# A two-layer transformer kernel on one core: new hand-made orders for every engine's work, with VectorE and GpSimd SBUF operations placed apart

## The reference, cut to what matters

```python
# layer 0: 8 query heads, 1 key/value head of 64, rotary embedding, SwiGLU of 2048
h = ada_rms(x, t, ln1_w, ln1_tw)        # n * (w * (1 + t @ tw.T))
q, k, v = h @ Wq.T, h @ Wk.T, h @ Wv.T
x = x + softmax(rope(q) @ rope(k).T / 8) @ v @ Wo.T
h = ada_rms(x, t, ln2_w, ln2_tw)
x = x + (silu(h @ Wg.T) * (h @ Wu.T)) @ Wd.T
# layer 1: 16 heads of 32, unit-length q and k, gates and shifts from the condition, GELU MLP of 2048
gamma1, gamma2, scale1, scale2, shift1, shift2 = silu(cond) @ Wada.T + bada
x = x + attn(_ln(x) * (scale1 + 1) + shift1) * gamma1
h = gelu_tanh((_ln(x) * (scale2 + 1) + shift2) @ Wfc1.T + bfc1)
x = x + (h @ Wfc2.T + bfc2) * gamma2
```

## Time and profile before

| | |
|---|---|
| median of 3 runs | 2560.11 us (2558.06 to 2566.29) |
| profiled execution | 2554.55 us, span 2552.8 us |
| mean granted clock of TensorE | 0.985 |
| busy: PE, DVE, ACT, POOL | 2449.8, 1422.2, 912.4, 1050.4 us |
| share of the DMA engines by the main queue | 35.8% |

### The profile page before, as it was taken

One profiled execution on the slowest core, in us unless ns is written; L12 is line 12 of the kernel. 1 busy time (PEld: TensorE's weight loads), 2 busy tenths in 40 slices (PEclk: granted clock), 3 DMA queues, 4 the chain that ended last, 5 costly groups with the idle time before them and its releaser, 6 DMA issues.

```text
span 2552.8 us, 46385 instructions
## 1 busy us (share of the span) xinstructions
PE 2449.8 (96%) x17878; PEld 1169.3 (46%) x17878; DVE 1422.2 (56%) x2062; ACT 912.4 (36%) x1496; POOL 1050.4 (41%) x943
## 2 busy tenths in 40 slices
...
GB/s 180 211 149 65 104 46 86 62 50 92 35 98 52 61 84 30 106 44 143 100 93 131 155 49 143 54 126 63 103 106 41 143 62 100 96 77 120 50 92 29
DMA packets 311504, 231.81 MB, mean 91 GB/s; under 512 B 227718, under 2 KB 238342, under 8 KB 311308
## 3 DMA queue, kind: packets, MB, share of 16 engines
q1 hardware_dynamic: 311308, 228.89, 35.8%
...
## 4 chain that ended last, share of the span: by engine, by line
PE 59%; POOL 16%; issue 12%; DVE 8%; ACT 3%; DMA 2%; SPq 1%; POOLq 0%; ACTq 0%; DVEq 0%
PE ps_m L1882 33%; PE ps_abef L1882 16%; POOL inner L1248 4%; PE ps_c L1882 3%; POOL scratch L1278 3%; POOL scratch L1274 3%; POOL scratch L1222 2%; POOL scratch L1284 1%; PE ps_d L1882 1%; DVE scratch L1845 1%; PE ps_abef L2105 1%; DMA inner<-tw_t 1%; DVE weights L1571 1%; ACT scratch L1505 1%; POOL x_attn L1287 1%
## 5 line engine op out<-in xcount | busy, mean ns | idle before, releaser
L1882 PE MATMUL ps_m<-h_mlp,weights 128*128 128x512 f16 x3168 | 736.4, 384 | 24.9 <-issue 8.5
L1882 PE MATMUL ps_m<-weights,inner 128*128 128x512 f16 x3072 | 679.3, 379 | 0.0
L1248 POOL TENSOR_TENSOR inner<-scratch,inner 128x512 f16<-128x512 f32 x256 | 322.4, 1264 | 489.8 <-ACT inner L1421 488.8
L1882 PEld LDWEIGHTS ps_m<-h_mlp,weights 128*128 128x128 f16 x3168 | 305.0, 99 | 395.2 <-issue 38.6
L1882 PEld LDWEIGHTS ps_m<-weights,inner 128*128 128x128 f16 x3072 | 298.1, 98 | 352.5 <-issue 0.2
L1882 PE MATMUL ps_abef<-h_mlp,weights 128*128 128x512 f16 x1440 | 329.0, 379 | 0.0
L1222 POOL TENSOR_TENSOR scratch<-scratch 128x512 f16<-128x512 f32 x120 | 163.1, 1359 | 340.2 <-ACT scratch L1374 340.2
L1882 PEld LDWEIGHTS ps_abef<-h_mlp,weights 128*128 128x128 f16 x1440 | 137.7, 98 | 165.6 <-issue 4.2
L1421 ACT CAST inner<-scratch 128x512 f16<-128x512 f32 x256 | 156.0, 613 | 121.8 <-DVE scratch L1716 64.4
L1374 ACT CAST scratch<-scratch 128x512 f16<-128x512 f32 x120 | 73.8, 615 | 334.3 <-DMA h_mlp<-scratch 189.3
L1845 DVE SCALAR_TENSOR_TENSOR scratch<-scratch 128x512 f32<-128x512 f32 x128 | 125.1, 978 | 61.2 <-ACT scratch L1510 61.2
...
## 6 DMA issues: line engine op xcount, KB each, us to landing
scratch<-mod SPq DMA_DIRECT2D x128, 256.0 KB, 4.0
...
weights<-gamma SPq DMA_DIRECT2D x128, 128.0 KB, 3.1
scratch<-scratch SPq DMA_DIRECT2D x128, 128.0 KB
scratch<-gain SPq DMA_DIRECT2D x112, 128.0 KB, 3.0
...
```

The lines of the kernel that those rows point to most:

```text
L1248: nc.gpsimd.tensor_tensor(inner[:, 1, j, :], src, inner[:, 0, j, :], ALU.subtract).then_inc(L.m_lo, 1)
L1882: ins = nc.tensor.matmul(o, left(a, k), right(b, k), start=(first and n == 0), stop=(last and n == len(order) - 1), skip_group_check=True)
```

## The change

Every plan table and every set-up list gets new numbers, hence a new order; nothing else in the kernel changes, and each engine has the same instructions as before. Some of the diff (all other entries of the tables change in the same way):

```diff
 SETUP0 = [
...
-    (26.66, "ada_ev", 0), (28.83, "ada_out", 0), (29.96, "rope", 1), (30.58, "cut", "wo"), (30.85, "sin", 2),
-    (34.03, "load", "ada5"), (44.15, "rope", 2), (46.98, "ada", 4), (49.69, "ada_ev", "g1"), (50.53, "sin", 3),
...
+    (-4.71, "bada", 0), (-3.60, "ada_out", 0), (3.06, "ada", "g1"), (3.30, "cut", "qkv"), (11.89, "cut", "qkv_v"),
...
+    (36.13, "ada_ev", "g1"), (36.58, "load", "ada5"), (41.40, "sin", 1), (47.53, "ada_ev", 1), (47.77, "ada", 4),
...
 STEADY1_AT = {
...
-    "sums": tiles([-12.82, 39.15, 70.71, 106.33]),
-    "v_lo": tiles([22.45, 38.41, 67.13, 100.48]),
-    "key_major": tiles([39.98, 71.78, 106.53, 150.49]),
-    "turn_p": tiles([41.55, 69.00, 102.86, 148.62]),
-    "mix": tiles([45.39, 73.02, 105.60, 159.76]),
...
+    "sums": tiles([-18.95, 36.55, 71.48, 107.75]),
+    "v_lo": tiles([4.04, 37.60, 70.69, 109.06]),
+    "key_major": tiles([40.70, 70.51, 112.78, 158.92]),
+    "turn_p": tiles([43.63, 68.97, 112.21, 169.30]),
+    "mix": tiles([46.07, 77.91, 116.14, 175.46]),
```

More of the change, by code:

```diff
@@ L110 @@
-    "spread": tiles([18.96, 70.34, 79.28, 104.72]),
-    "hi1": tiles([21.73, 33.52, 66.51, 103.23, 274.65]),
-    "shift": tiles([25.52, 57.20, 89.26, 103.72]),
-    "turn_p": tiles([26.00, 70.38, 91.99, 107.18]),
-    "p_lo": tiles([27.14, 67.60, 91.18, 108.70]),
-    "qk_hi": tiles([28.11, 65.13, 97.06, 113.78]),
-    "soft": tiles([30.57, 68.17, 93.96, 110.21]),
-    "scores": tiles([30.70, 50.42, 85.64, 103.46]),
-    "exp": tiles([35.79, 69.15, 105.65, 119.53]),
-    "mix": tiles([43.23, 78.98, 99.53, 181.77]),
@@ new lines @@
+    "lo1": tiles([-50.48, 31.04, 55.18, 91.55, 288.50]),
+    "proj": tiles([-46.96, 41.41, 77.48, 104.53]),
+    "turn": tiles([-27.43, 54.57, 75.15, 104.36]),
+    "qk_lo": tiles([-16.70, 43.74, 73.38, 96.46]),
+    "gain1": tiles([-2.95, 44.24, 59.42, 91.90]),
+    "spread": tiles([-2.40, 56.83, 92.18, 120.54]),
+    "hi1": tiles([12.55, 49.32, 74.46, 109.67, 268.70]),
+    "rot": tiles([23.11, 57.36, 84.21, 99.60]),
+    "scores": tiles([33.97, 74.51, 103.12, 145.10]),
+    "p_lo": tiles([34.57, 62.97, 91.99, 106.86]),
@@ new lines @@
+    "qk_hi": tiles([40.73, 59.51, 91.80, 121.91]),
+    "turn_p": tiles([42.01, 64.80, 103.50, 122.10]),
+    "shift": tiles([49.37, 73.78, 95.16, 140.93]),
+    "exp": tiles([50.27, 78.57, 110.00, 144.38]),
+    "p_hi": tiles([53.39, 85.05, 115.50, 148.71]),
+    "soft": tiles([56.09, 82.33, 98.98, 142.68]),
+    "mix": tiles([56.13, 80.02, 116.42, 171.89]),
+    "rstd2": tiles([56.14, 92.63, 148.08, 177.27]),
+    "out": tiles([62.19, 93.44, 143.07, 213.97]),
+    "c_lo": tiles([62.55, 87.70, 104.64, 200.54]),
@@ L137 @@
+    "fetch1": tiles([168.39], 4),
+    "flip1": tiles([215.34], 4),
+    "tables": tiles([233.20], 3),
 }
 STEADY0_AT = {
[L139 to L142 removed]
[4 rows of a table removed]
[L147 to L148 removed]
@@ new lines @@
+    "proj": tiles([13.38, 41.70, 49.06, 56.96]),
+    "hi1": tiles([15.22, 37.98, 50.68, 299.52], 1),
+    "shift": tiles([18.42, 50.35, 59.96, 104.54]),
+    "soft": tiles([21.44, 50.61, 72.30, 110.95]),
+    "flip1": tiles([23.30, 31.87, 50.37, 265.44], 1),
+    "p_lo": tiles([24.19, 58.01, 68.92, 90.74]),
+    "c_lo": tiles([25.34, 56.33, 94.76, 138.22]),
+    "exp": tiles([28.70, 53.07, 71.68, 114.39]),
+    "turn_p": tiles([31.45, 52.72, 94.15, 114.31]),
+    "scores": tiles([34.45, 53.86, 70.24, 108.69]),
@@ L208 @@
-    (52.53, "rope", 3), (55.45, "load", "ada6"), (55.50, "ada_ev", 1), (55.78, "cut", "gate0"), (58.26, "ada_ev", 4),
-    (63.46, "ada_out", 1), (66.47, "rows", 0), (68.27, "rope_out", 0), (68.42, "cut", "up0"), (71.64, "ada", 5),
-    (72.09, "load", "ada7"), (72.58, "ada_out", 4), (73.85, "ada", 6), (74.04, "ada_ev", 5), (76.17, "consts", 0),
-    (76.45, "ada_out", 5), (80.66, "load", "gate1"), (83.20, "ada_ev", 6), (87.64, "load", "ada2"),
-    (92.01, "bada", 1), (92.33, "ada", 7), (98.76, "ada", 2), (99.89, "ada_out", 6), (100.38, "load", "ada3"),
@@ L213 @@
[L213 to L216 removed]
+    (-159.02, "load", "ada4"), (-132.03, "ang", 0), (-73.55, "sin", 0), (-67.98, "ada", "g0"), (-67.07, "ang", 1),
```

422 lines of the change are left out of this document (202 added, 220 removed), and 119 rows, old and new, of tables (LAST1_AT, SETUP_START0, SETUP_START1, SETUP_TRANS).

## The result

| | before | after |
|---|---|---|
| median (4 runs each) | 2562.23 us (2558.06 to 2566.29) | 2504.68 us (2502.63 to 2506.86) |
| profiled execution | 2554.55 us, span 2552.8 | 2502.63 us, span 2500.8 |
| TensorE busy / idle in the span | 2449.8 / 103.0 | 2431.5 / 69.3 |
| mean granted clock of TensorE | 0.985 | 0.991 |

The span fell by 52.0 us. Of these 33.7 are idle time of TensorE, where the forecast's sum said 28.5. The other 18.3 are busy time with the same 17878 matmuls. Most of that is the clock, a term that the forecast had put at zero: by the granted clock over the whole span, TensorE lost 38.0 us to the lower level before and 22.5 after, 15.5 less.

A forecast was written before the change was run, and what follows sets the result against it. TensorE was taken to bound the kernel, with only its idle, about 100 us, removable. Layer 1 20, transition with first and last blocks 3.5, layer 0 0, set-up 5: 28.5 us off 2554.55 gives 2526, carried to the median 2531; range 2506 to 2562.

The forecast's parts named there:

- The clock: TensorE's granted clock, at 0.84 in the set-up: no gain taken, since no row shows it rising for less idle.
- (1): Layer 1, mix of tile 1: VectorE's sums 2 and v_lo 2 move behind key_major 1, gaining 2.5 us a block.
- (2): Layer 1, turn of tile 1: 14.1 us of cover instead of 12.8 against a 0.97 us wait, gaining 0.9 us.
- (3): Layer 1, turns of tiles 2 and 3: turn 3's 0.5 us gained in half the blocks, so 0.25 us.
- (4): Layer 1 block start: earlier out 3 and statistics gain 0.7 of 1.18 us; 1.56 us of issue wait stays.
- (5): Layer 1, new places with little room, such as turn 0 to scores 0: 1.0 us a block charged, between 0 and 4.
- Sum of a block: Steady layer 1 block: the five steps together gain 3.35 us, times six blocks 20 us, bounds 0 and 33.
- Layer 0: Layer 0's blocks: no idle to win, so 0, bounds 0 and 2 us a block, 16 us in all.
- rival (B): Slower: layer 0's mix 0 waits in each of eight blocks and other gains shrink; 2570 us, chance 0.13.
- Set-up: Set-up: 8 us gained at turn_x1 2, 3 us lost to a later ada5 load; 5 us, bounds -8 and +14.
- (C): More than forecast: layer 1 loses all but the issue wait, set-up gains 9, transition 8; 2510 us, chance 0.15.
- (D): The forecast itself, for the whole kernel: about 2531 us, own range 2518 to 2545, chance 0.57.

The follow-up runs named there:

- e5: Kernel before, with VectorE's v_lo and sums of tile 2 moved behind key_major of tile 1 in layer 1's steady blocks; 2543.78 us, ratio 0.9949.
- e12: e5 plus one ScalarE move: m_hi 11 behind its half of key_major 1; 2546.49 us, ratio 0.9949 to the kernel before.
- e13: Kernel before, with GpSimd's norm lo of tile 3 behind p_lo 1 and VectorE's scaling of tile 0 behind key_major 1; 2531.66 us, ratio 0.9898.
- e16: Kernel before, with one TensorE up step moved from behind scores 1 to ahead of turn 1 in layer 1's steady blocks; 2560.75 us, ratio 1.0006.
- e2: Kernel before, with only the changed kernel's tables for the first block and its set-up; 2554.67 us, ratio 0.9978.

## Why the prediction was right or wrong

The direction was right, and so were the places: all three waits that it named are gone or down to about a fifth, and layer 0 neither gained nor lost. The size was off by 28 us against the median: 18.3 of them are the busy time that it had at zero, 5.2 are idle time, and the other 5 or so come in because before's profiled execution, on which it was worked out, lay 7.7 us below its median and the changed kernel's only 2.1. By its own steps:

- **The clock, "I take no gain from it": the step that failed.** It measured 18.3 us of TensorE's busy time, of which 4.0 in the set-up and 14.0 from the transition through the three steady blocks. The argument was that no row shows it rising for less idle. The trace did, and the earlier trace rows hinted at it with 1.00 for one block and 0.99 for all: the block of 150.24 us was the cheapest of its kind. Mix 1 to mix 1, the next ones took 152.64 (1784.92 to 1937.56) and 153.50 us (to 2091.06), and the three steady blocks 458.17/3 = 152.7 on average, with the same instructions and nearly the same waits (the starts differ by up to 0.5 us). The rest of the difference is the slow stretches. The forecast's own mark, a period between 145 and 149 us, held by luck: after, it is 440.99/3 = 147.0 us, just what 150.24 - 3.35 gives, but a block gained 5.7 us and not 3.35, and the starting value was 152.7 and not 150.2. The two errors cancel there, and not in the sum.
- **(1) mix 1, 2.5 us a block: right size, wrong reason.** 2.64 us went, which is luck. "Of the meeting before it nothing has to go" fell with e5, e12 and e13: with the two steps moved and the meeting left, 1.57 us stayed; sums and v_lo could stay in front. Two producers had been left out, ScalarE's L1474, which hung on the same late gelu 11, and v_lo 2, which mix 1 needs done as it writes that bank.
- **(2) turn 1, 0.9: gone, but not a term by itself.** In e16 it came back whole at mix 1. In the changed kernel it counts, since mix 1 no longer waits.
- **(3) turn 3, 0.25:** 0.5. It waited 0.52 us in the block read, and none of L1745's 3 remaining waits lies in the three steady blocks.
- **(4) block start, 0.7: 0.2.** 2.74 us before, 2.72 after in the blocks shown, 8.8 and 8.2 in three, as "issue" rose by most of what the DMA wait fell. Why it rose is open.
- **(5) new tight places, charged 1.0:** 0.82, at turn 0 to scores 0. The other places cost nothing.
- **Sum of a block:** idle 22.3/3 = 7.4 to 10.6/3 = 3.5, so 3.9 for 3.35. From the transition to the end the idle fell by 2.5 + 7.3 + 11.7 + 6.8 = 28.3 us (forecast 23.5). By an estimate that gives the other block in the 7.3 its 3.9, transition and first block brought 6, not 3.5; two blocks at 3.9 account for the 6.8, so the last block's 0 holds.
- **Layer 0, 0:** right, rival (B) didn't come about; its idle went from 1.4 to 1.1 us.
- **Set-up, 8 - 3 = 5:** 9.1 in the profiled execution, 5.1 of it idle, and e2 gives 6 (1 to 11). Both terms were off and one was missing: the total is near the 5 by luck. L1629's waits fell to 3.8 us, not 10 to 14; ada5 made nobody wait; and turn_p 2 behind the loads of ada2 and its bias rows on SyncE made mix 2 wait 7.3 us. (A slip beside it: the upper bound's own terms, 8.95 and half of 12.2, make 15 and not 14.)
- **Range and chances:** (C), "all but the issue wait goes", came nearest, and it counted 50 us of idle and no clock. What happened was (D) and the clock. No case had the clock in it, so the range's lower end, 2506, was reckoned from idle time alone.
